# A layer walk that is written out six times, or once and then run as a loop on each compute engine

## The reference

```
x = x + attn_a(layernorm(x))     # 16 heads of 8, causal        stage A
x = x + ffn(layernorm(x))        # the stack of 6 layers        stage S0
x = x + attn_b(layernorm(x))     # 16 heads of 64, 4 groups     stage B
x = x + ffn(layernorm(x))        # the same stack again         stage S1
```

```
x = attn_layer(shift_tokens(x), Wqkv[i], ...) + x   # l2-normalised q, k; rotary; windows of 32 tokens
x = ffn_layer(shift_tokens(x), W1[i], W2[i], ...) + x   # layer norm, 341 * gelu(341), back to 128
```

## Time and profile before

| | |
|---|---|
| median of 3 runs | 6344.48 us (6340.2 to 6351.3) |
| the profiled execution | 6351.3 us, span of its instructions 6349.5 us |
| busy share of the span | PE 90%, PEld 62%, DVE 73%, ACT 53%, POOL 68% |
| mean granted PE clock | 0.963 |
| row_max of the first and of the last chunk of the stacks start at | 915.4 us and 6294.1 us |
| fetched instructions | q8: 604 packets, 9.90 MB; q14: 188 packets, 1.54 MB |

### The profile page before, as it was taken

One profiled execution on the slowest core, in us unless ns is written; L12 is line 12 of the kernel. 1 busy time (PEld: TensorE's weight loads), 2 busy tenths in 40 slices (PEclk: granted clock), 3 DMA queues, 4 the chain that ended last, 5 costly groups with the idle time before them and its releaser, 6 DMA issues. The chain is left out here.

```text
span 6349.5 us, 177383 instructions
## 1 busy us (share of the span) xinstructions
PE 5684.6 (90%) x76063; PEld 3936.3 (62%) x76063; DVE 4622.9 (73%) x6115; ACT 3391.7 (53%) x4021; POOL 4324.0 (68%) x2122
## 2 busy tenths in 40 slices
PE   7888978898989988889999999999688988889888
PEld 4444447676767776665555655554476776767675
DVE  6455448989989998675556565552588998888896
ACT  1444546666666666434444444434366666666664
POOL 2000048888888888427777777779688888888884
PEclk7889989999999999989999999999799999999999
DMA  0000012222222222100000000000122222222221
GB/s 25 1 2 1 2 45 63 76 63 73 69 68 74 69 70 63 47 1 1 1 1 1 1 1 1 1 1 1 51 63 70 66 76 66 72 67 68 61 69 48
DMA packets 188208, 253.46 MB, mean 40 GB/s; under 512 B 60828, under 2 KB 81816, under 8 KB 187288
## 3 DMA queue, kind: packets, MB, share of 16 engines
q1 hardware_dynamic: 187416, 242.03, 14.7%
HBM read 38.98 MB, written 1.57 MB: 6 GB/s over the span
## 5 line engine op out<-in xcount | busy, mean ns | idle before, releaser
L2092 POOL TENSOR_TENSOR XB<-XB,Pb 128x1024 f32<-128x1024 f32 x448 | 1070.6, 2390 | 338.6 <-ACT Pb L2052 297.5
L906 POOL TENSOR_TENSOR sin_qk<-raw_qk,rot 128x512 f32<-128x512 f32 x768 | 1001.1, 1325 | 11.5 <-ACT raw_qk L868 11.4
L922 POOL TENSOR_TENSOR rot_out<-rot_out,sin_qk 128x1024 f32<-128x1024 f32 x192 | 624.1, 3250 | 412.5 <-DVE rot_out L980 410.8
L2102 DVE TENSOR_REDUCE b_pmax<-slot 128x1 f32<-128x512 f32 x1024 | 653.4, 683 | 324.3 <-PE slot L1839 322.9
L2052 ACT ACTIVATE Pb<-slot 128x1024 f32<-128x1024 f32 x512 | 502.6, 1024 | 702.2 <-PE slot L1950 647.9
L939 POOL TENSOR_TENSOR inv_norm<-norm2c,minus_half 128x16 f32<-128x16 f32 x192 | 682.1, 3553 | 37.2 <-DVE norm2c L1081 23.0
L528 PE MATMUL slot<-w_hi,x_hi 128*128 128x512 f32 x1152 | 556.4, 483 | 120.1 <-DVE rot_out L980 63.4
L931 POOL TENSOR_TENSOR inv_norm<-norm2c,minus_half 128x16 f32<-128x16 f32 x192 | 558.8, 2911 | 55.3 <-DVE norm2c L1028 54.4
L786 ACT ACTIVATE V<-slot 128x1024 f32<-128x1024 f32 x192 | 196.6, 1024 | 598.2 <-PE slot L530 598.2
L1962 PE MATMUL slot<-Pb,Vb 128*64 128x512 f32 x2048 | 496.0, 605 | 1.1 <-ACT Pb L2052 1.1
L984 DVE TENSOR_TENSOR rot_out<-rot_out,inv_norm 128x1024 f32<-128x1024 f32 x384 | 479.5, 1249 | 5.9 <-POOL inv_norm L931 5.2
(11 more groups left out here) (213 smaller groups left out, 13361.7 us busy)
## 6 DMA issues: line engine op xcount, KB each, us to landing
VW<-V SPq DMA_DIRECT2D x1152, 128.0 KB, 2.4
VW<-V SPq DMA_DIRECT2D x768, 64.0 KB, 2.1
w_raw<-in_Wqkv SPq DMA_DIRECT2D x36, 512.0 KB, 3.7
Wo<-in_Wo SPq DMA_DIRECT2D x12, 512.0 KB, 4.4
W<-in_W SPq DMA_DIRECT2D x12, 341.0 KB, 3.2
consts<-in_shape_constants SPq DMA_DIRECT2D x1, 2436.5 KB, 9.2
QH<-rows_dram SPq DMA_DIRECT2D x128, 2.0 KB
QB<-rows_dram SPq DMA_DIRECT2D x128, 2.0 KB
```

The lines of the kernel that those rows point to most:

```text
L906: ins = pool.tensor_tensor(dst[:, :, x, :], src[:, :, 1 - x, :], tab, ALU.mult)
L922: pool.tensor_tensor(rot_out[0][:, :], rot_out[0][:, :], rot_sin[0], ALU.add)\
L2092: pool.tensor_tensor(b_sum[:, window % 2, :], Pb[:, (at - 1) % B_RING, :] if k == 1 else b_sum[:, window % 2, :], Pb[:, at % B_RING, :], A ...
L2102: dve.tensor_reduce(b_pmax[:, n // 2, u:u + 1], o[:, 512 * x:512 * x + 512], AX.X, ALU.max)\
```

## The change

In `read_steps` the first layer stays written out. Layers 1 to 5 become one body of 16 steps that is run five times, with the layer's number in a register L of each engine. The calls of `step` and what they issue are otherwise as before; `lo` is -EVER in all of layers 1 to 5 in both kernels.

```diff
         def read_steps(eng, call, step, longest):
 
-            for layer in range(DEPTH):
+            for k in range(NCH):
+                step(0, CHUNKS * call, BLOCKS * call, k, 0, EVER)
+            with eng.Fori(1, DEPTH) as L:
                 for k in range(NCH):
-                    step(layer, layer * NCH + CHUNKS * call, layer * NB + BLOCKS * call, k, -EVER if layer else 0, EVER)
+                    step(L, L * NCH + CHUNKS * call, L * NB + BLOCKS * call, k, -EVER, EVER)
             for k in range(longest):
                 step(DEPTH, CHUNKS * (call + 1), BLOCKS * (call + 1), k, -EVER, 0)
```

## The result

The changed kernel takes 6411.49 us (median of 5 runs, 6406.56 to 6420.70), the kernel before 6343.27 us beside it: a ratio of 1.0106, 95% interval 1.0093 to 1.0118. It is 68 us slower, where 126 were forecast.

The account below looks back on a forecast made before the run. It took a chain going back and forth between PE and DVE, both 90% busy, as the bound. Jumps 29 plus register instructions 96 gave 125 us on 6351.3, 6476, forecast 6470 us as the median is lower; 8-in-10 range 6375 to 6640.

Parts of the forecast that it names:

- likeliest case: Whole kernel: exposed jumps and register instructions together slow it to 6470 us, own range 6400 to 6560; chance 0.56.
- Busy times in the stacks unchanged: Sign in both stacks: engines' busy times stay the same and the extra time is all idle.
- a pause at every 16th step: Sign on PE, DVE, ACT and POOL: each pauses about 2.7 us where its loop jumps back.
- Term (a): Jumps back at 8 loop boundaries, 3.6 us each: 29 us, bounds 7 and 86.
- Term (b): Register instructions in 160 steps of layers 1 to 5, 0.6 us a step: 96 us, bounds 16 and 192.
- exposed time on DVE: Register instructions at DVE's own waits around q's and k's operations: 0.2 us for each, 0.4 us a step.
- A quarter of it will fall into waits that are there anyway: Register instructions: existing waits, DVE's 1.3 us for PE, cut 0.8 us a step to 0.6.
- The 0.2 us behind PE's small matmuls: On PE, one register instruction behind each of two groups of small matmuls: 0.2 us a step.
- the 32 us for hand-overs: Register instructions behind waits between PE, ACT and POOL, some two a step deciding anything: 0.2 us a step.
- Rival 1: Register instructions on other engines take twice SP's 0.10 us: 240 us plus 40 for jumps, 6625 us; chance 0.22.
- Rival 2: Register instructions all fall into the 10% idle time, only jumps of 7 to 29 us remain: about 6370 us; chance 0.16.
- Rival 3: PE's stops inside small matmuls, 124 us in 10 of 12 layers, vanish in the loop: 6243 us; chance 0.03.

Follow-up runs that it names:

- hint_all: The change with each loop's closing branch announced to the engine at the top of every pass; 38 us over the kernel before, ratio 1.0065.
- after_moved: The change with only PE's loop shifted so its unannounced closing branch lies near instruction 230 of a 256-instruction code block; 57 us over the kernel before, ratio 1.0086.
- hint_moved: hint_all with PE's loop shifted so its closing branch lies near instruction 230 of a 256-instruction code block; 37 us over the kernel before, ratio 1.0054.
- loop_not_pe: The change on DVE, ACT and POOL alone, PE written out as before; 30 us over the kernel before, ratio 1.0047.
- reg_all_nojump: The change's register instructions on all four engines, but all five layers written out in a body run once, without jumps; 30 us over the kernel before, ratio 1.0045.
- reg_dve_nojump: Only DVE keeps the layer in a register, nothing jumps, other engines written out as before; 18 us over the kernel before, ratio 1.0032.
- reg_pe_nojump: Only PE keeps the layer in a register, nothing jumps, other engines written out as before; -1 us over the kernel before, ratio 1.0010.
- nojump_waits_turned: reg_all_nojump with each group of waits in opposite order, so the wait that ends last stands on the instruction itself; 10 us over the kernel before, ratio 1.0014.
- late and early kernels: hint_waits_turned with PE's loop shifted, closing branch near instruction 230 (late) or 5 (early) of its 256-instruction block; 12 and 74 us over the kernel before.
- loop_pe: The change on PE alone, DVE, ACT and POOL written out as before; 55 us over the kernel before, ratio 1.0082.
- hint_waits_turned: The change with closing branches announced ahead and each group of waits in opposite order; 51 us over the kernel before, ratio 1.0092.

## Why the prediction was right, and where it was off

**The direction and the place.** Right. The added time lies in layers 1 to 5 (18.23 to 18.69 us a step, where 18.0 to 18.6 was written), stages A and B kept their length, and 6411 lies in the likeliest case's own range of 6400 to 6560, near its lower end. (That range does not follow from its parts: 6344 + 7 + 42 is 6393, and 42, 50 and 165 are not the bounds worked out before it.) "Busy times in the stacks unchanged" holds for all engines but PE, whose 30 us more the prediction did not have. Of the four engines that were each to show a pause at every 16th step only PE shows one that costs.

**Term (a), the jumps: 29 us.** The size was right: 30 us by the change against hint_all, 19 by after_moved against hint_moved. The working behind it was not. "The two engines that set the pace must both jump, so I take 2 x 2.7 - 1.8 = 3.6 us" does not hold: DVE's jump costs nothing that can be told from zero (loop_not_pe), and PE's alone makes the whole. It is also dearer than SP's 2.7 us, and PE's 1.8 us of idle time a step cover little of it: 22.7 us of idle time at L565 and 8.4 + 9.9 us of slower matmuls at L595 and L541 are 41 us, 5.1 a jump. That agrees with 36 to 44 us "at jumps" in the table; a quarter to a half of it is made up in the steps behind. The sum hit because two errors, one on either side, nearly cancelled.

**Term (b), the register instructions: 96 us.** This term was mis-sized: they cost 30 (reg_all_nojump). The price of one instruction behind a wait was right: 0.10 us forecast from the earlier trace rows, 134 - 35 = 99 ns measured on DVE. Of the exposed time on DVE, forecast at 0.4 us a step, half was there. For q the long operation starts 119 ns behind the end of the sum before and 346 ns in reg_dve_nojump (medians), 0.23 us more, or 36 us in all. For k it starts 460 ns behind the sum before and 346 in reg_dve_nojump, no later, since the short operation itself is shorter there (0.51 and 0.23 us by the medians). The step that failed is "A quarter of it will fall into waits that are there anyway". Of the 0.4 x 160 = 64 us forecast on DVE 18 arrived (reg_dve_nojump): nearly three quarters did not show. The profile had shown the cover, DVE's 1.3 us a step for PE, into which 0.4 us fit whole. In reg_dve_nojump this wait has shrunk from 283.8 us over the whole span to

```profile
DVE row_max L1007 <- PE slot L719: 256.1, 151, 3.5
```

The 0.2 us behind PE's small matmuls, 32 us, came to nothing (reg_pe_nojump, 0 to 13 us by its interval). Of the 32 us for hand-overs some 12 are there.

The model itself, that an instruction costs only behind the wait that ends last or behind a short operation, stands: 20 and 26 us of the register term go with the order of the waits alone, and the time behind q's short operation stays.

**The sum as measured.** By the steps from the change to hint_all, to reg_all_nojump, to nojump_waits_turned and to before: 30 for jumps, 8 for the named branches that remain and the place of the code (not split further), 20 for registers behind the last wait, 10 for registers elsewhere, 68 in all. Each of these differences is known to some 10 us, so the 8 and the 10 are rough.

**Rival 1, slow sequencers.** Wrong. DVE's register instructions take 46 ns, ACT's, POOL's and PE's 37, SP's 42: DVE is hardly slower than SP, and one behind a wait costs 0.10 us on DVE, not 0.20. The Trainium skill (Vector Engine (DVE) Microarchitecture Reference, Instruction fetch and dispatch) puts a short path for register operations in SP's sequencer alone; no run here shows a cost that would follow from that.

**Rival 2, hidden.** It lost, but it came nearer in size than its chance said: 6370 against 6411, with the forecast at 6470. Half of what it claims is true: three of four engines' jumps, PE's register instructions and most of DVE's are hidden.

**Rival 3, fewer stops.** Wrong: 149 us of stops in the small matmuls before, 155 after. The late and early kernels show that such stops do depend on where the code lies, so the rival had hold of something real, but worth tens of us and of either sign.

**A jump by the page.** The Trainium skill (Advanced Engine Details and Errata, Control Flow Timing) gives 108 ns for a compare-and-branch. Not taken, at the end of a loop, PE's takes 83 ns here, somewhat less. Taken, to code that is 11104 executed instructions back, it takes 3.6 to 4.3 us. Another page of the Trainium skill (Runtime: NRT & Kernel Launch, Instruction fetch mechanics) says that a taken branch out of the window that is held makes the engine wait for the page that it jumps to; it gives no price, and the runs agree with it in kind.

**What stays open.** Why loop_pe costs 55 us, when PE's registers cost about 0 and the jumps 19 to 30. Its steps at the jumps take 34 us more than reg_pe_nojump's; away from the jumps they are 0.13 us longer each, 18 us; the place of its code could do that, but no run moved it.

## What to carry to other kernels

Price a loop on the engine that sets the pace by its taken jump, idle and clock together, and name the branch ahead; then look in the trace whether it was really prepared, since a shift by 31 instructions turned 0.4 us into 4. Where a wait's value sits in a register, put the wait that ends last last, on the instruction itself. And before exposed time is added up, look at the idle time that the engine already has in the same step: where it was three times the forecast (1.3 against 0.4 us on DVE), little over a quarter came through, not three quarters.

## What the hardware showed that was not expected

- A taken jump far back holds PE's sequencer for 3.3 to 4.3 us, DVE's for 2.8 to 3.0, POOL's for 2.5 to 2.7, ACT's for 2.4 to 2.7 (these three in the change); named ahead at a good place, PE's for 0.4 to 0.5.
- Named ahead, with the branch at about instruction 5 of its 256, PE's took 3.5 to 4.1 us again at all eight jumps; at about 230, 0.4 to 0.5 at all eight.
- At 32 of 33 jumps with a pause of 1.8 to 3.4 us PE was granted 1.2 GHz for 3.4 to 10.2 us behind or around it. At the three with 1.2 to 1.7 us (hint_waits_turned), and at 27 of 28 with no pause, it stayed at 2.4 GHz.
- A register instruction takes 37 to 46 ns by the medians of the engines, but one between a wait and its instruction delays it by 99 ns.
- The same 18 us steps with the same instructions differed by 0.22 us a step (18.36 against 18.13, jumps and ends of loops left out) when PE's code was shifted by 31 instructions.
